# Attention of a macaron block: the last query tile's probabilities are turned by VectorE and a DRAM scratch instead of TensorE

## What is computed

```python
x = x + 0.5 * _L0_ffn_ref(_layernorm(x), ...)
x = x + _L0_attn_ref(_layernorm(x), W_Q, W_K, W_V, W_O)
x = x + 0.5 * _L0_ffn_ref(_layernorm(x), ...)

# attention
q, k, v = (einsum('ahe,bce->bach', W, x) for W in (W_Q, W_K, W_V))
scores = einsum('bach,baCh->bacC', k, q)
masked = where(tril, scores, -1e10)
attn = softmax(masked / 8)
z = einsum('bacC,baCh->bach', attn, v)
out = einsum('aeh,bach->bce', W_O, z)
```

## Time and profile before

| | before |
|---|---|
| runs | 969.61, 969.71, 970.89 us, median 969.71 |
| profiled execution | span 970.0 us, 24404 instructions |
| attention | from about 190 to 824 us of the span, 64 steps |
| busy over the span | PE 96%, PEld 82%, DVE 81%, ACT 74%, POOL 29% |
| DMA | 91.30 MB in 95935 packets |

### The profile page before, as it was taken

The page is one execution under the profiler, slowest core; times in us unless marked ns, Lnnn a source line. Parts: engine busy times, 40 slices in busy tenths (PEclk is TensorE's granted clock), DMA queues, the critical chain, the costliest instruction groups (busy, mean ns, idle before and its releaser), DMA issues.

```text
span 970.0 us, 24404 instructions
## 1 busy us (share of the span) xinstructions
PE 934.5 (96%) x7618; PEld 793.2 (82%) x7618; DVE 783.1 (81%) x3083; ACT 717.5 (74%) x2040; POOL 280.6 (29%) x328
## 2 busy tenths in 40 slices
PE   7899999899999999999999999999999999999994
PEld 6789999778787887878777787878778786999994
DVE  7878879688797788789789878978978987886666
ACT  3777667587878778787877878777877867787881
POOL 5777003322021012312221321310100111657551
PEclk9999999999999999999999999999999999999998
DMA  9678565121122122121112122111111113557757
GB/s 250 204 221 259 168 168 164 41 49 35 39 51 56 34 54 54 42 45 40 47 38 45 40 40 46 35 53 26 48 31 30 41 53 99 162 153 214 218 163 212
DMA packets 95935, 91.30 MB, mean 94 GB/s; under 512 B 30288, under 2 KB 71536, under 8 KB 95808
## 3 DMA queue, kind: packets, MB, share of 16 engines
q1 hardware_dynamic: 82896, 69.45, 25.7%
q0 software_dynamic: 8352, 18.17, 7.2%
q10 hardware_dynamic: 4560, 2.12, 0.8%
HBM read 64.50 MB, written 25.20 MB: 92 GB/s over the span
## 4 chain that ended last, share of the span: by engine, by line
PE 83%; DMA 4%; DVE 4%; issue 3%; POOL 2%; ACT 2%; SPq 1%; POOLq 0%; DVEq 0%; ACTq 0%
PE psum L2484 15%; PE psum L2473 14%; PE psum L2430 13%; PE psum L2315 9%; PE psum L2492 7%; PE psum L2266 7%; PE psum L2267 7%; PE psum L2268 7%; POOL x_slots L799 2%; PE psum L2278 1%; PE psum L2154 1%; PE psum L2288 1%; ACT arena L1073 1%; DMA arena<-x_slots 1%; DMA y_rows<-y_sb,y_tok 1%
## 5 line engine op out<-in xcount | busy, mean ns | idle before, releaser
L1073 ACT ACTIVATE arena<-arena,neg_max 128x512 f32<-128x512 f32 (+3 forms) x512 | 281.1, 556 | 1.6 <-DVE neg_max L1900 1.6
L1900 DVE CUSTOM_DVE_ANT_0 arena<-psum,causal 128x512 f32<-128x512 f32 (+3 forms) x512 | 217.2, 482 | 3.0 <-PE psum L2430 3.0
L1081 ACT ACTIVATE arena<-psum 128x512 f32<-128x512 f32 x192 | 107.8, 596 | 140.6 <-PE psum L2473 140.6
L2484 PE MATMUL psum<-arena 128*64 128x512 f32 (+3 forms) x1024 | 152.0, 439 | 0.7 <-DVE arena L1913 0.7
L2473 PE MATMUL psum<-ident,arena 128*128 128x128 f32 x1280 | 150.5, 273 | 1.1 <-ACT arena L1073 0.7
L1016 ACT ACTIVATE arena<-psum,b_t 128x256 f32<-128x256 f32 (+1 forms) x336 | 120.9, 444 | 35.6 <-PE psum L2268 26.5
L818 POOL DMA_INDIRECT arena<-y_tiles,y_at x64 | 61.2, 956 | 290.8 <-PE psum L2430 207.1
L2473 PEld LDWEIGHTS psum<-ident,arena 128*128 128x128 f32 x1280 | 141.9, 141 | 1.7 <-ACT arena L1073 1.1
L2315 PE MATMUL psum<-w_sb,arena 128*128 x1136 | 140.8, 275 | 0.4 <-DVE y_sb L1770 0.3
L2484 PEld LDWEIGHTS psum<-arena 128*64 128x64 f32 x1024 | 68.0, 136 | 83.9 <-issue 74.1
L799 POOL DMA_INDIRECT x_slots<-xr,slot x64 | 62.1, 970 | 252.8 <-PE psum L2430 206.9
(11 more groups left out here) (358 smaller groups left out, 1897.4 us busy)
## 6 DMA issues: line engine op xcount, KB each, us to landing
arena<-inv_dram SPq DMA_DIRECT2D x128, 128.0 KB, 2.9
w_raw<-in_L_ffn_W_dram SPq DMA_DIRECT2D x60, 256.0 KB
xg<-x_slots SPq DMA_DIRECT2D x43, 144.0 KB
arena<-in_L_ffn_W_dram SPq DMA_DIRECT2D x24, 256.0 KB
arena<-y_rows SPq DMA_DIRECT2D x16, 256.0 KB, 4.7
y_tiles<-y_sb SPq DMA_DIRECT2D x27, 128.0 KB, 2.2
x_slots<-blank SPq DMA_DIRECT2D x18, 144.0 KB
arena<-x_slots SPq DMA_DIRECT2D x15, 144.0 KB
```

The costliest lines, as they stand in the source:

```text
L1073: ins = act.activation(prob_tile(i, h, t), prob_tile(i, h, t), ACT.Exp, scale=-1.0, bias=neg_max[i % 2][:, h, t:t + 1], accum_out=row_sum[ ...
L1081: act.activation(four_turned(g), turned_bank(i, g), ACT.Copy).then_inc(pt_act, 1)
L1900: ins = dve.tensor_tensor_reduce(out=prob_tile(i, h, t), in0=score_tile(t, h), in1=causal[:, SEQ - (t + 1) * P:SEQ], scale=-1.0, scalar=-2 ...
L2484: ins = pe.matmul(RING_C[m, k * P:SEQ], v_sb[i // V_PAIRS % 2][:, k, col:col + DH], probs_t[:, h * 10 * P + PT_COL[k]:h * 10 * P + PT_COL[ ...
```

## The change

In steps 0 to 62 the eight squares of the last query tile (t = 3, k = 0..3, two heads) are no longer turned by TensorE. Instead:

- VectorE's `turn_long(i)` transposes `probs` tile 3 of both heads, 128 x 512 each, in blocks of 32 x 32 within the same 32 partitions, and writes them to `turned`. It stands behind the maxima of step i. It waits for `exps(i, 0)` and for the store of the step before.
- SyncE's `turn_long(i)` stores `turned` (512 KB) to a DRAM scratch in four DMAs, one for each group of 32 partitions, in runs of 1 KB; waits until all have landed; waits for `attend(i - 1)`; and loads it back in one DMA, 4 KB to a partition, into `late_t` (the last four places of the `y_sb` ring). It stands ahead of `spread_sums(i)`.
- TensorE turns 12 squares in three groups, all copied by ScalarE; VectorE's two copies go. `attend` has six matmuls for tiles 0 to 2 (384, 256 and 128 columns, two heads) and then eight of 128 columns for tile 3, ahead of which it waits for the load (`late_loaded`).
- The order changes: VectorE's `invert(i - 1)` stands ahead of `maxima(i, 0)`; ScalarE's `exps(i, 0)` stands ahead of the copies; TensorE's `project_q(i + 1)` stands right behind `project_k(i + 1)`, ahead of `project_v`.
- The last step, 63, turns all 20 squares on TensorE as before. Some start-up semaphores are merged into one counter.

```diff
+            def turn_long(i):                      # SyncE
+                par = i % 2
+                sp.wait_ge(turned_ready, i + 1)
+                wait(sp, late_loaded, 16 * (i - 1))
+                rows = turned_dram[par].rearrange("(j r) (g e) -> g r j e", r=BLOCK, e=EACH)
+                for g in range(P // BLOCK):
+                    sp.dma_start(rows[g], turned[g * BLOCK:(g + 1) * BLOCK, :].rearrange("r (j e) -> r j e", e=EACH)).then_inc(turned_stored, 16)
+                sp.wait_ge(turned_stored, stored_long(i + 1))
...
+                wait(sp, z_ps, i)
+                sp.dma_start(late_t, turned_dram[par]).then_inc(late_loaded, 16)
...
             for i in range(STEPS):
+                if i < STEPS - 1:
+                    turn_long(i)
                 spread_sums(i)
...
             def transposed(i):                     # ScalarE
                 wait(act, z_ps, i)
-                for g in (0, 2, 3):
+                for g in (0, 1, 2) if i < STEPS - 1 else (0, 2, 3):
...
+                    exps(i, 0, [3])
                     if i > 0:
                         transposed(i - 1)
...
-                    exps(i, 0, [3])
...
+            def turn_long(i):                      # VectorE
+                dve.wait_ge(exp_done, S_USES * i + 1)
+                wait(dve, turned_stored, stored_long(i))
+                for h in range(2):
+                    ins = dve.transpose(long_block(h), prob_tile(i, h, QT - 1).rearrange("p (k j s) -> p k j s", k=QT, s=BLOCK))
+                ins.then_inc(turned_ready, 1)
...
-                    maxima(i, 0, [3])
                     if i > 0:
                         invert(i - 1)
+                    maxima(i, 0, [3])
                     maxima(i, 1, [2])
                     maxima(i, 2, [1, 0])
-                    if i > 0:
-                        transposed(i - 1, 1)
-                        transposed(i - 1, 4)
+                    if i < STEPS - 1:
+                        turn_long(i)
...
             def transposes(i):                     # TensorE
-                squares = [(h, k, t) for h in range(2) for k in range(QT) for t in range(k, QT)]
-                for g in range(5):
+                squares = [(h, k, t) for h in range(2) for k in range(QT - 1) for t in range(k, QT - 1)]
+                if i == STEPS - 1:
+                    squares += [(h, k, QT - 1) for h in range(2) for k in range(QT)]
+                for g in range(len(squares) // 4):
...
             def attend(i):
+                for k in range(QT - 1):
+                    for h in range(2):
+                        m = slice(h * DH, (h + 1) * DH)
+                        pe.matmul(RING_C[m, k * P:(QT - 1) * P], value(k, h), probs_t[...], start=(k == 0), stop=False)
+                if i == STEPS - 1:
+                    pe.wait_ge(pt_dve, 2)
+                else:
+                    pe.wait_ge(late_loaded, 16 * (i + 1))
                 for k in range(QT):
                     for h in range(2):
                         m = slice(h * DH, (h + 1) * DH)
+                        ins = pe.matmul(RING_C[m, (QT - 1) * P:SEQ], value(k, h), late_square(i, h, k), start=False, stop=(k == QT - 1))
...
                     if i + 1 < STEPS:
                         project_k(i + 1)
+                        project_q(i + 1)
                     pe.wait_ge(max_ready, S_USES * (i + 1))
                     if i + QT - 1 < STEPS:
                         project_v(i + QT - 1, RING_B)
```

More of the change, by code:

```diff
@@ L55, in macaron_block_kernel @@
     R = 2
+    BLOCK = 32
     TS = R * P
@@ L199, in macaron_block_kernel @@
         xh = [sb(f"xh{i}", [D, P]) for i in range(2)]
-        y_sb = [sb(f"y_sb{i}", [P, R, D]) for i in range(YRING)]
+        y_all = sb("y_all", [P, YRING * R * D])
+        y_sb = [y_all[:, i * R * D:(i + 1) * R * D].rearrange("p (r d) -> p r d", r=R) for i in range(YRING)]
         class Lots:
@@ L222, in macaron_block_kernel @@
         P_COL = [0, P, 3 * P, 6 * P]
-        PT_COL = [0, 4 * P, 7 * P, 9 * P]
+        PT_COL = [0, 3 * P, 5 * P]
         probs = [[lot(10 * P) for h in range(2)] for i in range(2)]
         probs_t = lot(20 * P)
+        turned = probs_t[:, 12 * P:20 * P]
+        EACH = 2 * QT * BLOCK
+        LATE_IN = range(YRING - P // BLOCK * EACH // (R * D), YRING)
+        late_t = y_all[:, LATE_IN.start * R * D:]
         v_sb = [lot(QT * 4 * P).rearrange("p (k m) -> p k m", k=QT) for i in range(2)]
@@ L389, in macaron_block_kernel @@
         w2_loaded = sem("w2_loaded")
-        ident_zero, ident_ready = sem("ident_zero"), sem("ident_ready")
         const_ready = sem("const_ready")
-        numbered = sem("numbered")
+        IDENT_ZERO, IDENT, NUMBERED, ZEROED, MASKS_BEGUN, ALL_READY = range(1, 7)
         centre_ps, centred = sem("centre_ps"), sem("centred")
@@ L474, in macaron_block_kernel @@
         inv_loaded = [sem(f"inv_loaded{i}") for i in range(2)]
+        turned_ready = sem("turned_ready")
+        turned_stored = sem("turned_stored")
+        late_loaded = sem("late_loaded")
         pt_ps = sem("pt_ps")
@@ L559, in turned_bank, with stored_long, long_block, late_square @@
                 return (RING_B, RING_A, RING_C, RING_B, RING_A)[g]
-            return (RING_C, LONG[0], LONG[1], K_BANK if i == STEPS - 2 else Q_BANK, RING_C)[g]
+            return (RING_C, *LONG)[g]
         def four_turned(g):
             return probs_t[:, g * 4 * P:(g + 1) * 4 * P]
+        def stored_long(steps):
+            return 16 * P // BLOCK * steps
+        def long_block(h):
+            return turned.rearrange("p (j h k s) -> p h k j s", h=2, k=QT, s=BLOCK)[:, h]
+        def late_square(i, h, k):
+            if i == STEPS - 1:
+                return turned[:, (h * QT + k) * P:(h * QT + k + 1) * P]
+            return late_t.rearrange("p (g h k s) -> p h k g s", h=2, k=QT, s=BLOCK)[:, h, k]
         def route_step(b):
@@ L708, in spread_sums @@
                     ).then_inc(inv_loaded[par], 16)
+            def turn_long(i):
[6 more added lines that the diff above has]
+                sp.wait_ge(turned_stored, stored_long(i + 1))
+                if i == 0:
+                    for j in LATE_IN:
+                        sp.wait_ge(y_stored[j], stored(last_in_place(j, NTS[0])))
+                wait(sp, z_ps, i)
+                sp.dma_start(late_t, turned_dram[par]).then_inc(late_loaded, 16)
             load_first_tiles()
@@ L962, in negate @@
             def negate():
-                act.wait_ge(ident_ready, 1)
+                act.wait_ge(const_ready, IDENT)
                 for i, by in enumerate((-1.0 / SCALE, -1.0)):
@@ L1908, in invert, with last_transposed @@
                 dve.reciprocal(inv_sum[i % 2][:, :, :], row_sum[i % 2][:, :, :]).then_inc(inv_ready, 1)
-            def transposed(i, g):
+            def turn_long(i):
[4 more added lines that the diff above has]
+                ins.then_inc(turned_ready, 1)
+            def last_transposed(g):
+                i = STEPS - 1
                 dve.wait_ge(pt_ps, PT_USES * i + g + 1)
                 wait(dve, z_ps, i)
+                if g == 4:
+                    dve.wait_ge(turned_stored, stored_long(i))
                 dve.tensor_copy(four_turned(g), turned_bank(i, g)).then_inc(pt_dve, 1)
@@ L2058, in attention @@
                 invert(STEPS - 1)
-                transposed(STEPS - 1, 1)
+                last_transposed(1)
                 finish(work)
-                transposed(STEPS - 1, 4)
+                last_transposed(4)
                 finish(seek_tiles(1))
@@ L2114, in split_some @@
                     yield
-            dve.wait_ge(numbered, 1)
+            dve.wait_ge(const_ready, NUMBERED)
             name_tiles()
@@ L2123, in _ @@
             finish(unit_moments(0, 0))
-            dve.wait_ge(const_ready, 2)
+            dve.wait_ge(const_ready, MASKS_BEGUN)
             dve.wait_ge(router_w_loaded, 32)
@@ L2133, in _ @@
             side_by_side(split_some(6, 8), place_rows(2, bank[4]))
-            dve.wait_ge(const_ready, 3)
+            dve.wait_ge(const_ready, ALL_READY)
             dve.wait_ge(w2_loaded, 32)
@@ L2478, in attend, with value @@
                 pe.wait_ge(pt_act, PT_ACT * (i + 1))
-                pe.wait_ge(pt_dve, PT_DVE * (i + 1))
+                def value(k, h):
+                    col = i % V_PAIRS * P + h * DH
+                    return v_sb[i // V_PAIRS % 2][:, k, col:col + DH]
+                for k in range(QT - 1):
+                    for h in range(2):
+                        m = slice(h * DH, (h + 1) * DH)
+                        pe.matmul(RING_C[m, k * P:(QT - 1) * P], value(k, h),
+                                  probs_t[:, h * 6 * P + PT_COL[k]:h * 6 * P + PT_COL[k] + (QT - 1 - k) * P], start=(k == 0), stop=False)
+                if i == STEPS - 1:
+                    pe.wait_ge(pt_dve, 2)
+                else:
+                    pe.wait_ge(late_loaded, 16 * (i + 1))
                 for k in range(QT):
```

(5 more changed lines are left out.)

26 lines of the change are left out of this document (11 added, 15 removed).

## The result

The changed kernel took 985.2 to 992.88 us in four runs, a median of 989.16, against 970.06 for the kernel before: a ratio of 1.0186 (95% interval 1.0163 to 1.0209). It is 1.9% slower where 3% faster was forecast. The measured 989 lies inside the range of 925 to 1003, on the side of rival 1, the string of DMAs on SP.

The account below looks back on a forecast made before the run. The prediction took PE to bound the kernel at 9.91 us a step. Loops of 9.19, 9.25 and 9.35 gave a step of 9.45, saving 0.46 us in 63 steps, 29 us: 941.0 us, range 925 to 1003.

Parts of the forecast that it names:

- rival 1: SP's DMAs exceed the old 9.91 us step through slow stores or an inverse store waiting out the load: 1007 us, chance 0.28.
- PE's part: TensorE: eight of twenty transposes go, -0.87 us a step; attend's smaller passes add 0.15; loop 9.19 us.
- The cut of attend: In attend on TensorE, 8 pairs of passes become 14, costing between 0 and 0.38 us; 0.15 taken.
- The loop of ACT and DVE: ScalarE's work of 7.54 us, invert, tile 3's maxima and handovers close a loop: 9.06 us plain, 9.25 with extras.
- DVE: VectorE: two copies of 0.690 us go, two 128 x 512 transposes come at 0.69; busy 8.2 of about 9.3 us.
- SP's string: SyncE's DMAs and waits of one attention step, worked off in order: 9.35 us, from 7.7 to 11.2.
- Load and inverse store: On SyncE, the 512 KB load with the inverse store behind it: 3.0 us without queueing, up to 1.7 more; 3.8 taken.
- Stores: SyncE's four stores of the turned blocks, 512 KB, from issue to landing: 4.15 us, from 3.45 to 5.15.
- Inverse loads and handovers: On SyncE, issuing two inverse loads takes 1.08 us and four handovers 0.3 us a step.
- I take 3.8: The value in us chosen for SyncE's load with the inverse store behind it, between no queueing and full queueing.
- the string is as long as the step that PE and ACT would allow: SyncE's DMAs at 9.35 us match the engines' loops; the load's own landing costs nothing, but the length counts.
- Three loops within 0.2 us of each other: Loops of TensorE 9.19, ScalarE with VectorE 9.25 and SyncE 9.35 us give an attention step of 9.45.

## Why the prediction was wrong

- **PE's part** was right. From the first transpose of a step to the first projection it is 1.25 us for twelve against 2.10 for twenty: 0.85 saved, 0.87 forecast. The cut of attend, priced at 0.15, cost next to nothing: from 419.67 to the scores at 421.99 it is 2.32 us, against 2.31, the lower bound of 0.
- **The loop of ACT and DVE** was priced at 9.06 plain and 9.25 with extras. Without the DMAs the step is 9.15, and there the chain of waits runs over ACT and DVE (36% and 22% of the span), as the prediction has it. But PE is busy for 299.5 of 300 us in that run, and its loop was priced at 9.19. So neither loop is above 9.15, and the run doesn't size them apart.
- **DVE**: the transposes took what the copy took, 0.69 us. The row, from 300 to 600 us:

```profile
L1959 DVE STREAM_TRANSPOSE arena<-arena 128x512 f32<-128x512 f32 x58 | 37.7, 688 | 0.6 <-DMA turned_dram<-arena 0.6
```

- **SP's string** was the right mechanism with three terms too small. Load and inverse store: 3.8 forecast, 0.39 + 4.01 = 4.4 measured in the median and 4.3 in the mean; of the up to 1.7 us that the load could add, about 1.3 came (4.01 against 2.73). Stores: 4.15 forecast, 4.33 in the median and 4.48 in the mean; the four issues take 2.0 us together instead of 1.5. Inverse loads and handovers: 1.08 and 0.3 forecast, 1.19 in the median and 1.48 in the mean, since an issue takes up to 2.5 us. Together 9.35 forecast, 9.92 by the medians and 10.26 by the means, and the step is 10.27.
- **The step that failed** is "I take 3.8", with "the string is as long as the step that PE and ACT would allow". Three loops within 0.2 us of each other were called even, and the one with landings that scatter was given its middle value. The term measured 4.3 to 4.4, the largest of the three misses: 512 KB were known to stand ahead of the inverse store. And a string without slack passes every late landing on, so its mean counts, not its median. So the string alone set the step, at 10.27, and all that PE had gained was lost behind it.
- **Rival 1** had the mechanism, the point from which it decides and the sign: DVE waits for the inverse loads in nearly every step. Its 1007 was too far (10.5 a step against 10.27), with a chance of 0.28. That 989 lies inside the range is owed to this rival, not to the forecast.

## What to carry to other kernels

Where a change adds a large transfer to a queue that also carries small ones that somebody waits for, price the small ones with the large one's bytes ahead of them, add up the whole string between two rounds, and ask for slack against the new, shorter step. Here the engines' loops and the string were forecast even, and the string, whose terms scatter, was the longest. Then put the small transfer first: here that one move turned 1.9% slower into 2.8% faster. Another queue is no substitute, since the small store issued behind the load on it waited just as long. An order taken from a changed kernel isn't good or bad by itself: the changed kernel has the two new orders and reaches 9.15 us a step without its DMAs, and the kernel before, where a bank is used twice, loses 3% by them.

## What the runs showed of the hardware

- From its issue to the next issue that waits for it, a 4 KB store takes 2.7 us with no large transfer beside it, 3.05 ahead of a 512 KB load, 3.07 behind one of 128 KB, and 3.84 to 4.01 behind one of 512 KB on the same queue (medians). From another engine's queue it takes 2.96 to 3.16 when issued ahead of that load and 4.20 to 4.25 when issued behind it.
- Issuing a DMA isn't of fixed cost: the stores' issues have a median of 0.45 us and a maximum of 1.8, those of the inverse loads 0.56 and 2.5, though nothing in the instruction changes.
- A transpose on VectorE of 128 x 512 float32 in blocks of 32 costs 0.69 us, as a copy of that size out of PSUM does.
- One kernel took 970 us on one chip and 1032 on two others, and the changed kernel's ratio to it was 1.019 in the result and 1.009 on chip 0.
